# A two-layer attention and expert kernel: parts of the projections made on GpSimd, layer 1's projections moved six beats earlier, layer 0's first queries before the keys, zero fills merged

## What is computed

```python
x = L0_attn_x
xn = _layernorm(x, axis=-1)
s = _L0_attn_ref(xn, ...)      # differential attention: 16 heads, 2 maps each, 4 key heads, rope
g = _silu(_L0_ffn_ref(xn, ...))  # 16 experts, top 2, and 2 shared ones
x = x + s * g
xn = _layernorm(x, axis=-1)
s = _L1_attn_ref(xn, ...)      # 16 heads, rope, causal
g = _silu(_L1_ffn_ref(xn, ...))  # 8 experts, top 1, at most 160 tokens each
x = x + s * g
```

## Time and profile before

| | us |
|---|---|
| runs before | 589.54, 584.73, 586.56; median 586.56 |
| the profiled execution, its own time | 581.26 |
| its span, first to last instruction | 579.5 |
| PE busy | 446.1 (77%) |
| DVE busy | 319.2 (55%) |
| ACT busy | 198.9 (34%) |
| POOL busy | 172.4 (30%) |
| mean granted PE clock | 0.882 |

### The profile page before, as it was taken

How to read it: one execution, slowest core, us unless ns; L and a number is a source line. 1 busy time by engine, 2 the same in 40 slices (tenths; PEclk the granted TensorE clock), 3 DMA queues, 4 the chain that set the end, 5 groups by cost and what they waited for, 6 DMA issues and landing times.

```text
span 579.5 us, 10279 instructions
## 1 busy us (share of the span) xinstructions
PE 446.1 (77%) x3600; PEld 307.9 (53%) x3600; DVE 319.2 (55%) x831; ACT 198.9 (34%) x427; POOL 172.4 (30%) x204
## 2 busy tenths in 40 slices
PE   3437689869889998799999997739547387489961
PEld 3314466635665564477777774527435265367540
DVE  3746347769788764145422358766726276351435
ACT  1100234434364555633433232312113224145222
POOL 2310110206466414022000174234204355130224
PEclk9757779989999999999999998977757879699985
DMA  6288797765236300423332341250552935600204
GB/s 216 59 136 277 258 274 197 207 159 94 82 117 137 70 1 3 128 83 101 109 92 84 109 154 36 65 100 28 155 113 85 204 102 120 146 3 2 68 25 145
DMA packets 50572, 65.87 MB, mean 114 GB/s; under 512 B 8131, under 2 KB 41795, under 8 KB 48987
## 3 DMA queue, kind: packets, MB, share of 16 engines
q1 hardware_dynamic: 48219, 58.93, 38.9%
q0 software_dynamic: 2304, 6.29, 3.5%
HBM read 42.88 MB, written 22.02 MB: 112 GB/s over the span
## 4 chain that ended last, share of the span: by engine, by line
PE 52%; DVE 18%; issue 12%; DMA 8%; POOL 3%; SPq 3%; ACT 2%; POOLq 0%; DVEq 0%; ACTq 0%
PE bank L998 8%; PE bank L1020 6%; PE bank L796 5%; PE bank L893 4%; DVE work L1460 4%; PE bank L827 4%; PE bank L900 3%; PE bank L823 3%; DMA work<-parts 3%; PE bank L943 3%; PE bank L921 3%; DMA k_parts<-work 2%; PE bank L851 2%; DVE work L1424 2%; PE bank L1005 2%
## 5 line engine op out<-in xcount | busy, mean ns | idle before, releaser
L1460 DVE TENSOR_REDUCE work<-bank 128x4 f32<-128x512 f32 (+1 forms) x144 | 96.6, 687 | 92.8 <-PE bank L827 90.3
L1122 ACT ACTIVATE work<-bank 128x512 f32<-128x512 f32 x144 | 84.2, 594 | 98.8 <-PE bank L851 55.2
L823 PE MATMUL bank<-neg_ts,identb 128*128 128x512 bf16 (+1 forms) x144 | 50.9, 353 | 66.8 <-issue 41.4
L1085 ACT ACTIVATE work<-bank 128x256 f32<-128x256 f32 (+4 forms) x131 | 51.5, 401 | 90.3 <-PE bank L867 44.9
L823 PEld LDWEIGHTS bank<-neg_ts,identb 128*128 128x128 bf16 x144 | 15.3, 106 | 87.2 <-issue 81.9
L827 PE MATMUL bank<-work 96*128 96x256 bf16 (+1 forms) x320 | 51.7, 269 | 0.0
L1250 POOL TENSOR_TENSOR work<-work 128x512 f32<-128x512 f32 (+1 forms) x20 | 21.3, 1063 | 101.3 <-ACT work L1085 101.2
L900 PE MATMUL bank<-work,cst 128*32 128x256 f32 (+1 forms) x768 | 50.5, 333 | 0.0
L1241 POOL TENSOR_SCALAR_AFFINE_SELECT work<-work 128x256 f32<-128x256 f32 (+1 forms) x48 | 23.2, 488 | 89.6 <-ACT work L1122 85.0
L1020 PE MATMUL bank<-moe,work 88*128 (+1 forms) x188 | 49.8, 388 | 0.0
L1763 DVE TENSOR_TENSOR work<-work,bank 128x176 f32<-128x176 f32 x47 | 15.8, 337 | 59.5 <-ACT work L1175 59.2
(11 more groups left out here) (195 smaller groups left out, 761.6 us busy)
## 6 DMA issues: line engine op xcount, KB each, us to landing
moe<-w_in SPq DMA_DIRECT2D x27, 352.0 KB, 6.0
work<-q_parts SPq DMA_DIRECT2D x48, 128.0 KB, 4.5
x_slots<-wo SPq DMA_DIRECT2D x41, 128.0 KB, 2.4
work<-x_slots SPq DMA_DIRECT2D x31, 128.0 KB, 2.2
y_slots<-work SPq DMA_DIRECT2D x31, 128.0 KB, 1.7
q_parts<-work SPq DMA_DIRECT2D x8, 384.0 KB, 3.2
parts<-work SPq DMA_DIRECT2D x8, 384.0 KB, 2.6
moe<-f1a_in SPq DMA_DIRECT2D x4, 512.0 KB, 4.0
```

The source lines that it names most:

```text
L823: nc.tensor.matmul(view[:, :, half * P:half * P + P], identb[:, :], neg_ts[:, :].unsqueeze(1).to_broadcast([P, len(ms), P]), start=True, s ...
L1085: return nc.scalar.activation(dst, src, ACT.Copy)
L1122: nc.scalar.activation(pT[at % 6], a.st.bank(w)[:, :], ACT.Exp, scale=SCALE)\
L1460: nc.vector.tensor_reduce(here[:, first:first + len(ms), half], a.s.bank((b, q))[:, :].rearrange("p (m s) -> p m s", s=n), AX_X, ALU.max, ...
```

## The change

- A pair has six steps. mid and low go into rest: POOL does the three operations one behind the other, and the copy to the middle part is made by POOL in place of ACT.
- In layer 0 the first queries are pair 0 of a batch and the keys pair 1 (`key_side`); the beats of the three pairs and of the first four settle steps move.
- In layer 1 all steps of the pairs of batches 1 to 3 stand six beats earlier (`ahead`).
- The zero fills are made in eleven bulk items of up to four tiles, twelve transfers (one item crosses from the one buffer to the other). Layer 0's bulk starts at beat 30, one item every second beat. Layer 1's f1 weights become bulk items of their own, from beat 13 on, one every third beat.

```diff
-    dict(x=(0, 16, 30, 31), settle=(5, 5, 7, 11, 15, 18, 20, 26),
-         pairs=((1, 2, 3, 4, 5, 6, 8, 11), (4, 5, 6, 7, 8, 9, 11, 13), (9, 10, 11, 12, 13, 14, 16, 18)), kept=(13, 14),
-         bulk=18,
+    dict(x=(0, 16, 30, 31), settle=(7, 9, 11, 13, 15, 18, 20, 26),
+         pairs=((1, 2, 3, 4, 6, 8), (3, 4, 5, 6, 8, 10), (9, 10, 11, 12, 14, 16)), ahead=0, kept=(13, 14),
+         bulk=(30, 2),
...
-         pairs=((0, 0, 1, 1, 2, 2, 3, 4), (2, 2, 3, 3, 4, 4, 5, 6)), kept=(4, 4),
+         pairs=((0, 0, 1, 1, 2, 3), (2, 2, 3, 3, 4, 5)), ahead=6, kept=(4, 4),
+         bulk=(13, 3),
...
-PAIR_STEPS = ("project", "turn", "high", "rest", "mid", "low", "stage", "load")
+PAIR_STEPS = ("project", "turn", "high", "rest", "stage", "load")
...
+FILLS = -(-(SLOT_TILES0 + SLOT_TILES1) // 4) + (SLOT_TILES0 % 4 > 0)
...
+BULK = (BULK0, [(kind, e, 2) for kind in ("first", "second") for e in range(0, E1, 2)])
...
-                        put(here + beat, kind, (b, g))
+                        put(here + beat - (c["ahead"] if b else 0), kind, (b, g))
...
-            for k in range(len(BULK) if n == 0 else 0):
-                put(c["bulk"] + k, "bulk", (k, c["bulk"] + k - c["maxima"]))
+            for k in range(len(BULK[n])):
+                beat = c["bulk"][0] + k * c["bulk"][1]
+                put(beat, "bulk", (k, beat - c["maxima"]))
...
+                if kind in ("first", "second"):
+                    dst, src = ((f1a, f1a_d), (f1b, f1b_d))[kind == "second"]
+                    sp.dma_start(dst[:, at:at + n], src[:, at:at + n]).then_inc(ld["f1"], 16)
...
-                    for j in range(at, at + n):
-                        slots_d, row = (x0_slots_d, j * P) if j < SLOT_TILES0 else (x1_slots_d, (j - SLOT_TILES0) * P)
-                        sp.dma_start(slots_d[row:row + P, :], zeros).then_inc(filled, 16)
+                    for slots_d, first, end in ((x0_slots_d, 0, SLOT_TILES0), (x1_slots_d, SLOT_TILES0, SLOT_TILES0 + SLOT_TILES1)):
+                        j0, j1 = max(at, first), min(at + n, end)
+                        if j0 < j1:
+                            sp.dma_start(slots_d[(j0 - first) * P:(j1 - first) * P, :].rearrange("(j p) d -> p j d", p=P),
+                                         zeros.unsqueeze(1).to_broadcast([P, j1 - j0, D])).then_inc(filled, 16)
...
-                        at = a.shares * w[0] + w[1]
-                        if at < 4:
-                            for dst, src in ((f1a, f1a_d), (f1b, f1b_d)):
-                                sp.dma_start(dst[:, 2 * at:2 * at + 2], src[:, 2 * at:2 * at + 2]).then_inc(ld["f1"], 16)
...
-                key, col = ("pair", b, g), 2 * P * g
+                key, col = ("pair", b, g), 2 * P * (g if a.n else (1, 0, 2)[g])
...
-                        if kind == "rest":
-                            pool.wait_ge(a.high, n + 1)
-                            nc.gpsimd.tensor_tensor(whole, whole, split[n % 2][:, 0, 0:width], ALU.subtract).then_inc(a.rest, 1)
-                        else:
-                            pool.wait_ge(a.mid, n + 1)
-                            nc.gpsimd.tensor_tensor(split[n % 2][:, 2, 0:width], whole, split[n % 2][:, 1, 0:width],
-                                                    ALU.subtract).then_inc(a.parted, 1)
+                        high, mid, low = (split[n % 2][:, k, 0:width] for k in range(PARTS))
+                        pool.wait_ge(a.high, n + 1)
+                        nc.gpsimd.tensor_tensor(whole, whole, high, ALU.subtract).then_inc(a.rest, 1)
+                        pool.wait_ge(a.rest, n + 1)
+                        nc.gpsimd.tensor_copy(mid, whole).then_inc(a.mid, 1)
+                        pool.wait_ge(a.mid, n + 1)
+                        nc.gpsimd.tensor_tensor(low, whole, mid, ALU.subtract).then_inc(a.parted, 1)
```

More of the change, by code:

```diff
@@ L522, in pair_at, with query_at, query_side @@
             return a.first + a.sides * b + g
+        def query_at(a, g):
+            return g // 2
+        def query_side(a, m):
+            return 2 * (m // 16) if a.n == 0 else 1
         def pair_width(a, g):
-            return SEQ if a.n == 0 and g == 0 else 2 * SEQ
+            return SEQ if (a.n, g) == (0, a.key_side) else 2 * SEQ
         def pair_maps(a, g):
-            return (a.maps, a.groups) if g == 0 else (16 * g - 16, 16 * g)
+            q = query_at(a, g)
+            return (a.maps, a.groups) if g == a.key_side else (16 * q, 16 * q + 16)
         def parts_home(a, b, g):
@@ L535, in parts_home @@
                 return parts1_d[2 * b + g]
-            return q0_parts_d[2 * b + g - 1] if g else k0_parts_d[b]
+            return k0_parts_d[b] if g == a.key_side else q0_parts_d[2 * b + query_at(a, g)]
         def max_use(a, q):
@@ L677, in load @@
                 if b >= a.kept:
-                    last = 4 * g - 1 if a.n == 0 and g else a.units - 1
+                    last = 3 if (a.n, g) == (0, 0) else a.units - 1
                     sp.wait_ge(a.st.full, a.st.at[(b - a.kept, last, 2)] + 1)
                 rows = qkT[a.n][b % a.kept][0:STACK, m0:m1, :].rearrange("p m t -> p (m t)")
-                if g == 0:
+                if g == a.key_side:
                     for r0, times in ((0, 3), (3, 2), (5, 1)):
@@ L697, in attention @@
                         sp.wait_ge(a.s.full, w[1])
-                        bulk(*BULK[w[0]])
+                        bulk(*BULK[a.n][w[0]])
                     elif kind == "rows" and a.n == 0:
@@ L814, in scores @@
                 qk = qkT[a.n][b % a.kept]
-                for g in (0, 1 + ms[-1] // 16):
-                    pe.wait_ge(a.loaded[b % 2][g], 16 * (6 if g else PARTS) * (b // 2 + 1))
+                for g, times in ((a.key_side, PARTS), (query_side(a, ms[-1]), 6)):
+                    pe.wait_ge(a.loaded[b % 2][g], 16 * times * (b // 2 + 1))
                 if a.n == 0 and (b, q) == (0, a.by_share[0]):
@@ L1100, in attention @@
                         nc.scalar.activation(sc[:, 1, :], sc[:, 0, :], ACT.Exp).then_inc(norms[a.n].expd, 1)
-                    elif kind in ("high", "mid"):
+                    elif kind == "high":
                         n, width = pair_at(a, *w), pair_width(a, w[1])
-                        act.wait_ge(a.turned if kind == "high" else a.rest, n + 1)
-                        copy(split[n % 2][:, int(kind == "mid"), 0:width],
-                             rotated[n % 2].rearrange("p c t -> p (c t)")[:, 0:width]).then_inc(a.high if kind == "high" else a.mid, 1)
+                        act.wait_ge(a.turned, n + 1)
+                        copy(split[n % 2][:, 0, 0:width], rotated[n % 2].rearrange("p c t -> p (c t)")[:, 0:width]).then_inc(a.high, 1)
                     elif kind == "rows":
```

13 lines of the change are left out of this document (7 added, 6 removed).

## The result

The changed kernel takes **557.2 us** (median of 4 runs, 553.3 to 559.6) against 585.8 (4 runs, 584.7 to 589.5): a ratio of 0.949, 95% interval 0.942 to 0.957. That is faster, by 28.6 us and not by the 42.9 of the forecast; 557.2 lies inside the range of 528 to 567 and 13.5 us above the forecast of 543.7. The profiled execution took 553.3 us, the fastest of its four.

What follows compares the result with a forecast made beforehand. PE sets the pace except at latency gaps. Terms 31.5 + 13.9 + 3 - 1.5 - 2 - 2 = 42.9 us gained: 538.4 from the profiled 581.26, 543.7 against the median 586.56; range 528 to 567.

Steps and rivals of the forecast that it cites:

- Layer 0, 13.9: Layer 0's attention: first score 1.9 us earlier and PE gaps of 2.59, 4.09 and 5.36 gone, 13.9 us gained.
- the loads still come late: Rival: stores and loads slow beside f1 and zero fills; only 21 us gained, 565 us; chance 0.15.
- The zero fills' price of 2 us: Layer 0: zero fills run beside batch 1's stores and loads, 2 us lost (0 to 6).
- Layer 1, 31.5: Layer 1, first scores of batches 1 to 3: 14 beats ahead (29.8 us) cover 27.6 us latency, 31.5 us gained.
- The front, net 0: Layer 1's start: last normalization 7 to 10 us late, some 7 us of projections gone; 2 gained to 3 lost.
- the mark that was to show the prediction wrong: Layer 1's last normalization over 10 us later against the experts' end would show the forecast wrong.
- 1.5 for masking: Masking of probabilities queues behind GpSimd's three-part runs and PE's value products wait: 1.5 us lost (0 to 4).
- POOL's copy, 0.65: GpSimd's added middle-part copy over 128x512 takes 0.65 us, at most 1.15.
- DVE paying for a busier POOL, 2 us: Twenty copies hold GpSimd 13 us longer and slow VectorE's steps: 2 us lost (0 to 7).
- The clock, 3 us: With all seven gaps closed, PE runs less at 1.2 GHz in place of 2.4: 3 us gained (0 to 9).
- the last rival: Layer 1's early projections push router and batch 1 back 10 us, nothing recovered: 550 us, inside the range; no separate chance.
- the rival of a dear conversion: GpSimd's copy far dearer; two fit a batch until about 5.2 us each; at 8 us, 602 us; chance 0.03.

Runs made afterwards that it cites:

- e1: Changed kernel with layer 0's third-pair load moved from beat 16 to 18, behind the row-maxima transfers: 547.1 us, ratio 0.935.
- e2: Changed kernel with layer 0's bulk loads at beats 44 to 81, one every beat, in place of every second from 30: 557.9 us, ratio 0.952.
- e7: Kernel before the change with only the six beats ahead in layer 1 added: 568.0 us, ratio 0.970.
- e4: Changed kernel with layer 1's projections not moved ahead (0 beats in place of 6): 562.1 us, ratio 0.962.
- e8: Changed kernel without the six beats ahead and with f1 loaded in twos behind rows steps as before: 572.0 us, ratio 0.978.
- e9: Changed kernel, six beats kept, with f1 loaded in twos behind layer 1's first four rows steps as before: 560.3 us, ratio 0.961.
- e5: e1 with layer 1's beats 6 to 8 (batch 1's first steps) run after the experts' rounds: 545.6 us, ratio 0.934.
- e6: e1 with the middle part copied by ScalarE in place of GpSimd: 545.5 us, ratio 0.933.
- e10: e1 with three beats ahead in layer 1 in place of six: 558.4 us, ratio 0.956.
- e11: e10 with the middle part copied by ScalarE in place of GpSimd: 555.6 us, ratio 0.952.
- e12: e10 with layer 1's second-pair load moved from 5 to 8, behind the rows: 546.3 us, ratio 0.937.

## Why the prediction was right in its sign and too high in its size

**Sign and cause: right.** The gaps were latency; the change closed the three of layer 1 and cut those of layer 0 to under 2 us or to nothing.

**Layer 0, 13.9: the failed step.** The experts started 4.1 us earlier and not 10 to 15. Its own four terms came out: first score 2.8 us earlier (1.9 forecast), 2.59 gone, 4.09 cut by 2.4, 5.36 by 4.1, in sum 11.9. DVE waited for no store of parts any more, and batch 0's rows were issued at 55.15, 0.6 us after their transposition (54.56). But the prediction counted what a load on SP makes wait ("rows, bulk and the next store queue behind it; exponentials wait for those rows, four beats or more later") and gave it no cost. That was said of layer 1, where the six beats leave room; in layer 0 the third load had moved from behind the rows of beat 42 to two beats ahead of them, and no sentence followed it there. It cost about 8 us (e1 against after, by waits and by the means of layer 0's end; 10 by the medians). What it cost was not the wait for the store, which ended before the rows were ready, but the issue of the loads and of the bulk transfer behind them (the rows left 1.3 to 1.6 us late) and their transfers, behind which the rows landed in 5.3 to 6.0 us in place of 1.8. The rival "the loads still come late" put 6 us of layer 0 at risk, but at the scores; it was the rows behind the loads that were late. The zero fills' price of 2 us has its place here: at the first wait e2, without them beside the store, took 1.38 in place of 4.30, but lost more at the second.

**Layer 1, 31.5: the gaps closed, but not by the six beats alone.** All 31.5 were put down to the six beats. They alone brought 17 of before's time (e7: 585.2 to 568.0), 17.0 from the logits to the end by the profile, where the whole change brought 26.8. The other 9.7 came with the parts that were costed as no gain, f1's singles and the shorter way to the load (e4, e8); how they share it beside the six beats is open (e9). That the time fell well inside the range is in part luck: without these uncosted parts it would stand near its end, some 567 (an estimate: 557.2 and 9.7). The step that failed took the 27.6 us of latency as fixed, where other parts of the change shorten it. With it unshortened, as in e7, 14 beats do close the first scores, and the loads then hold the rows back.

**The front, net 0: 3.0 lost,** the bound named. The last normalization began at 393.73 in place of 387.42, with the experts' rounds 4 us earlier: some 10 us late, at the mark that was to show the prediction wrong, but the logits came only 3 late. What stood there moved elsewhere when it was taken out (e5).

**New waits in layer 1, 1.5 for masking.** POOL's masking held PE once, for 2.56 us. Not foreseen was that the waits on DVE behind the first row maxima of a batch would grow, from 2.93 and 2.85 to 4.41, 2.44 and 1.93: DVE turns the next pair there. The six beats closed 16.8 us of gaps and are worth 5 us by the medians (e4), 7.9 by the spans (559.5 to 551.6). The front took most of the difference: PE's waits there are 5.65 in e4 (1.60 and 4.05) and 10.47 after (2.25 and 8.22), 4.8 more. The waits within the batches (those of 1.2 us and more, without the three gaps) are 9.3 in e4 and 11.3 after, 2.0 more. The rest is not explained.

**POOL's copy, 0.65: right.** Its line, grouped over the execution of after (count: shortest, median and longest in ns):

```profile
L1266 POOL CAST work<-work x20: 396/609/687, 18.3 to 453.3; 128x512 bf16<-128x512 f32 x16, 128x256 bf16<-128x256 f32 x4
```

**DVE paying for a busier POOL, 2 us.** DVE's busy time grew by 5.3 (319.2 to 324.5); the three pairs of runs put 1.6 to 4.1 of it on the path by the medians and 0.9 to 2.5 by the ratios. The size agrees; that it is on the path is argued, not shown. Two instructions of DVE in after where it is seen, and the two of POOL beside them:

```profile
420.08 1.38 DVE L1442 TENSOR_TENSOR work<-work 128x256 f32<-128x256 f32 x1
422.86 1.08 DVE L1486 TENSOR_TENSOR work<-work 128x16 f32<-128x16 f32 x1
```

```profile
420.03 1.15 POOL L1268 TENSOR_TENSOR work<-work 128x512 bf16<-128x512 f32 x1
422.76 1.15 POOL L1264 TENSOR_TENSOR work<-work 128x512 f32<-128x512 f32 x1 [0.48 <-ACT work L1100]
```

The operations of these two lines take 0.43 and 0.19 us in the median; here they last until POOL's subtraction ends or a little longer. The rule of the Trainium skill (SBUF, State Buffer, section Who interferes with whom), an exclusive lock on the ports that both engines share, agrees with these lines.

**The clock, 3 us,** can't be separated: the mean granted clock rose from 0.882 to 0.896, and PE's busy time fell by 3.5 us.

**Two side sums** are off without touching the forecast. In the last rival, 10 us on top of 543.7 are 553.7 and not 550. In the rival of a dear conversion, 15.06 of 26.1 us leave 11.0 for two copies, 5.5 each and not 5.2.

**What stays open:** the last wait for rows in layer 0 (3.0 to 4.4 us in e1, e5, e6, e10, e11 and e12), whose transfer runs beside the experts' weights; no run moved it. Nor did a run part the loads' issue from their transfers in layer 0, or the loads from the bulk transfer behind them: moving the load takes all of it away.

## What to carry to other kernels

A load can make small transfers behind it late in three ways: by waiting on the queue for its data (5.2 us in e10), by its own issue (1.3 to 2.7 us), and by the bytes that then go ahead, its own and those of what stood behind it (5.3 to 6.0 us to land in place of 1.8). So when one is moved, list what it passes, above all small transfers with a reader close by, and compare three times for each: when it was ready, when it was issued, when it landed. Put the load behind them, even where its data are then ready later; here that was worth 10 to 12 us, twice, for one number each. A gap that is a latency has several parts that can each be shortened, so take the edits of a change away one at a time before the gain is put down to one of them.

## What the hardware showed that was not expected

How long a 384 KB store to DRAM takes until its load can go out depended on its neighbours by a factor of three: 2.6 us alone (e10, 388.73 to 391.33), 6.0 right behind three loads and with a 512 KB transfer issued behind it (e10, 392.61 to 398.57), 6.2 beside zero fills (after, 70.21 to 76.41), 8.9 behind two 512 KB transfers and three loads (e7, 434.05 to 442.95). Rows of 8 KB depended on theirs as much: 1.8 us to land with the six loads behind them (e1), 5.3 to 6.0 with the loads and a bulk transfer ahead (after), 6.3 behind the experts' weights (e1, issued at 183.38). And layer 0's attention, with the same instructions, ended 3.5 us apart in two executions (240.07 and 243.59), so a single profile does not settle a step of that size.
